# Three norms' rows on ScalarE, the key's gate as a scale of the turned probabilities, the feature shift on ScalarE

## The reference

```python
# part a: a state-space block, ends in a layer norm
y = y * silu(z)
y = y * rsqrt(mean(y * y) + EPS) * norm_w
y = einsum('bld,ed->ble', y, out_proj_w) + x
x = (y - mu) * rsqrt(var + EPS) * ln_w + ln_b        # "ln1"; the residual and "ln2" follow
# part b: attention, 8 heads of 64; the value is the one expert's whose gate is greatest,
# times that gate g[token, head]; the output is mixed by experts and scaled by the query's gate
out = softmax(q @ k.T * scale, causal) @ (g * v_expert)
x = layernorm(out_mixed + x)                           # "lnB"
# part c: linear attention with rotary angles
q, k = gelu(x @ Wq + bq) + 0.21, gelu(x @ Wk + bk) + 0.21
x = layernorm(rope(q) @ (rope(k).T @ v) / z + x) * gamma + beta   # "lnC"; residual and "lnD" follow
```

## Time and profile before

| | |
|---|---|
| median of 3 runs | 1579.16 us (1578.62 to 1583.59) |
| the profiled execution | 1580.04 us, its span 1578.1 us |
| mean granted TensorE clock | 0.974 |
| TensorE busy | 1438.5 us, 91% |
| VectorE busy | 1214.6 us, 77% |
| ScalarE busy | 820.8 us, 52% |
| GpSimd busy | 790.4 us, 50% |
| token stage, expert stage | 0 to 1068.6 us, 1068.6 to 1578.1 us |

### The profile page before, as it was taken

The page is one execution under the profiler, slowest core; times in us unless marked ns, Lnnn a source line. Parts: engine busy times, 40 slices in busy tenths (PEclk is TensorE's granted clock), DMA queues, the critical chain, the costliest instruction groups (busy, mean ns, idle before and its releaser), DMA issues. The chain is left out here.

```text
span 1578.1 us, 32322 instructions
## 1 busy us (share of the span) xinstructions
PE 1438.5 (91%) x10752; PEld 1261.2 (80%) x10752; DVE 1214.6 (77%) x2335; ACT 820.8 (52%) x1846; POOL 790.4 (50%) x1959
## 2 busy tenths in 40 slices
PE   5588999999999999999999999946999999869997
PEld 4366788788788788788788787836999999869997
DVE  4466798898898898898898887764888888736664
ACT  2234544544544544544544544303777776557774
POOL 0332253553553553553553552222777777557763
PEclk9998999999999999999999999966999999989999
DMA  6000000000000000000000000008676667877782
GB/s 236 7 7 1 8 1 14 15 1 14 15 1 15 15 1 14 15 1 15 15 1 15 8 1 8 8 7 252 171 197 188 185 186 199 254 266 301 300 316 71
DMA packets 140752, 132.10 MB, mean 84 GB/s; under 512 B 7376, under 2 KB 130512, under 8 KB 134096
## 3 DMA queue, kind: packets, MB, share of 16 engines
q1 hardware_dynamic: 140624, 130.50, 26.1%
HBM read 73.85 MB, written 56.62 MB: 83 GB/s over the span
## 5 line engine op out<-in xcount | busy, mean ns | idle before, releaser
L636 PE MATMUL bk<-ve_f,oe 128*128 128x128 f32 x2048 | 275.8, 279 | 0.8 <-DVE ve_f L1360 0.8
L636 PEld LDWEIGHTS bk<-ve_f,oe 128*128 128x128 f32 x2048 | 248.9, 192 | 23.4 <-issue 20.1
L2287 POOL TENSOR_TENSOR d_s<-d_ex 128x1024 f32<-128x1024 f32 x32 | 131.8, 4120 | 100.8 <-ACT d_ex L2087 100.8
L1360 DVE SCALAR_TENSOR_TENSOR ve_f<-ps_m,oT 128x512 f32<-128x512 f32 x248 | 166.3, 678 | 3.7 <-PE bk L636 2.3
L1321 DVE COPY_PREDICATED vals<-oh,bk 128x1024 f32<-128x1024 int32 x112 | 146.6, 1309 | 10.3 <-PE bk L404 8.5
L2037 PE MATMUL d_sl<-d_ex,e_prT 128*128 128x128 f32 x1024 | 136.0, 277 | 8.8 <-POOL d_ex L2304 8.8
L1971 PE MATMUL d_lg<-d_phf,d_xtf 128*128 (+1 forms) x1024 | 128.1, 287 | 14.4 <-DVE d_ex L2191 7.6
L1971 PEld LDWEIGHTS d_lg<-d_phf,d_xtf 128*128 128x128 f32 x1024 | 125.1, 203 | 15.2 <-issue 11.1
L2037 PEld LDWEIGHTS d_sl<-d_ex,e_prT 128*128 128x128 f32 x1024 | 125.4, 193 | 9.0 <-POOL d_ex L2304 9.0
L1981 PE MATMUL d_sl<-d_ex,d_xs 128*128 128x128 f32 x1024 | 121.3, 277 | 5.8 <-DVE d_ex L2202 5.8
L1981 PEld LDWEIGHTS d_sl<-d_ex,d_xs 128*128 128x128 f32 x1024 | 118.4, 194 | 6.2 <-DVE d_ex L2202 6.2
(11 more groups left out here) (340 smaller groups left out, 3730.5 us busy)
## 6 DMA issues: line engine op xcount, KB each, us to landing
logits<-d_raw SPq DMA_DIRECT2D x128, 256.0 KB, 3.3
e_lt<-logits SPq DMA_DIRECT2D x32, 1024.0 KB, 5.1
y_slots<-d_ys SPq DMA_DIRECT2D x64, 256.0 KB, 4.3
d_ex<-y_slots SPq DMA_DIRECT2D x16, 1024.0 KB, 6.8
d_w<-W SPq DMA_DIRECT2D x16, 256.0 KB, 3.4
oe<-xT SPq DMA_DIRECT2D x1, 2048.0 KB, 7.9
xt_in<-xT SPq DMA_DIRECT2D x16, 128.0 KB, 2.3
x_in<-x SPq DMA_DIRECT2D x16, 128.0 KB, 2.4
```

The lines of the kernel that those rows point to most:

```text
L636: last = pe.matmul(ps_u[:, cols], oe[:, hp, e, :], mo[:, n % MO, hp, :], start=False, stop=(e == NE - 1 and hp == HP - 1), skip_group_chec ...
L1360: V.scalar_tensor_tensor(mo[:, n % MO, :, :].rearrange("p a n -> p (a n)"), chosen_of(b, c), float(NE - e), oT[:, u, c, :, :].rearrange("p ...
L2287: G.tensor_tensor(s8[:], part[:, 0:8, :], part[:, 8:16, :], ALU.add).then_inc(n, 1)
```

## The change

The rows of three of the norms (ln1, lnB, lnC) are made by ScalarE. VectorE makes -mean * rstd (`shift`, one 128x2 instruction a norm), and ScalarE computes Identity(x * rstd + shift) in two instructions of 128x128. VectorE goes on with the product behind the rows when ScalarE has made them. The gate of the key isn't multiplied into vals by GpSimd (`b_vg` is gone) but is the scale of `b_pt`, which is now two instructions, 128x256 and 128x128. `c_q` is on ScalarE, behind the Gelus. Some buffers share space: sz is tz, yg is ya, and six buffers of the preparation lie in lx and mx; two waits move with that.

```diff
+        nb = {n: sb(f"{n}_b", [C]) for n in ("ln1", "lnB", "lnC")}
...
-        def scale_rows(dve, n, src, dst, b):
-            wait(dve, norms[n]["rstd"], RSQRT_OPS * (b + 1))
+        def shift(dve, n, b):
+            dve.wait_ge(norms[n]["rstd"], RSQRT_OPS * (b + 1))
+            dve.scalar_tensor_tensor(nb[n][:], nbuf[n][1][:, :, 0], -1.0, rstd_of(n)[:], ALU.mult, ALU.mult
+                                     ).then_inc(norms[n]["shift"], 1)
+        def scale_rows(act, n, src, dst, b):
+            act.wait_ge(norms[n]["shift"], b + 1)
             for c in range(C):
-                dve.tensor_scalar(dst[:, c, :], src[:, c, :], nbuf[n][1][:, c, 0:1], rstd_of(n)[:, c:c + 1],
-                                  ALU.subtract, ALU.mult).then_inc(norms[n]["rows"], 1)
+                nc.scalar.activation(dst[:, c, :], src[:, c, :], ACT.Identity, scale=rstd_of(n)[:, c:c + 1],
+                                     bias=nb[n][:, c:c + 1]).then_inc(norms[n]["rows"], 1)
...
@@ TensorE, b_pv @@
-                    pe.wait_ge(q["b_vg"], C * (b + 1))
+                    pe.wait_ge(q["b_v"], (NE - 1) * (b + 1))
...
@@ ScalarE @@
             def a_tz(b):
-                wait(act, q["a_sz"], b)
+                wait(act, q["a_yg"], b)
...
             def b_pt(b, h):
-                copy(pt[:, s, a, :, :].rearrange("p a b -> p (a b)"), ps_v[0][:, a, 0:3 * P]
-                     ).then_inc(q["b_pt"], 1)
+                nc.scalar.activation(pt[:, s, a, 0:2, :].rearrange("p a b -> p (a b)"), ps_v[0][:, a, 0:2 * P], ACT.Copy,
+                                     scale=gx[:, 0, h:h + 1])
+                nc.scalar.activation(pt[:, s, a, 2, :], ps_v[0][:, a, 2 * P:3 * P], ACT.Copy, scale=gx[:, 1, h:h + 1]
+                                     ).then_inc(q["b_pt"], 1)
...
+            def c_q(b):
+                act.wait_ge(q["c_g"], 2 * (b + 1))
+                wait(act, q["c_out_ps"], b)
+                nc.scalar.activation(ql[:], gl[:], ACT.Copy, bias=SHIFT).then_inc(q["c_q"], 1)
...
@@ ScalarE, slot @@
                     a_st(t)
                 if c:
+                    b_x2(t - 3, 1 - u)
                     b_x2t(t - 3, 1 - u)
...
                     c_gelu(t - 3)
+                    c_q(t - 3)
                 if more:
                     a_cin(t + 1, 0)
...
                     b_probs(t - 1, 3)
+                if a:
+                    a_na(t)
                 if more:
                     a_tz(t + 1)
...
                     b_probs(t - 1, 5)
+                if c:
+                    c_ncn(t - 3)
+                if b:
                     b_rgs(t - 1, 1)
...
@@ VectorE @@
             def a_y(b):
                 dve.wait_ge(q["a_y_ps"], b + 1)
+                wait(dve, q["a_sq"], C * b)
+                wait(dve, q["a_yt_ps"], b)
...
             def a_ln1(b):
-                scale_rows(dve, "ln1", ra, na, b)
                 dve.wait_ge(norms["ln1"]["rows"], C * (b + 1))
...
             def b_gate(b):
+                wait(dve, q["b_pt"], HB * b)
                 V.tensor_reduce(gx[:], g[:], AX.X, ALU.max).then_inc(n, 1)
...
             def c_ln(b):
-                scale_rows(dve, "lnC", rc2, ncn, b)
                 dve.wait_ge(norms["lnC"]["rows"], C * (b + 1))
...
@@ VectorE, slot @@
                     b_v(t - 1, 1)
                 if c:
-                    b_x2(t - 3, 1 - u)
+                    shift(dve, "lnB", t - 3)
...
                     b_v(t - 1, 6)
-                if c:
-                    c_q(t - 3)
...
                     b_max(t - 1, 1)
+                if a:
+                    shift(dve, "ln1", t)
                 if o:
                     b_mo(t - 2, u, 0, 7)
                 if a:
                     a_ln1(t)
...
                     b_mo(t - 2, u, 1, 1)
+                if c:
+                    shift(dve, "lnC", t - 3)
                 if b:
                     b_max(t - 1, 2)
                     b_rg(t - 1, 1)
...
@@ GpSimd, slot @@
                     rsqrt(pool, "rms", t, 1.0 / DI, EPS, q["a_sq"], C)
-                if b:
-                    b_vg(t - 1)
```

More of the change, by code:

```diff
@@ L117, in token_blocks @@
         causal_s = sb("causal_s", [P])
-        negb_f = sb("negb_f", [3, P])
         negb = sb("negb", [3, P], BF16)
@@ L129, in token_blocks @@
         in_w = sb("in_w", [2 * DI + 2 * D + NH])
-        out_w0 = sb("out_w0", [2, D])
         out_w = sb("out_w", [2, D])
@@ L165, in token_blocks @@
         bet = sb("bet", [D])
[L168 to L173, removed]
         ea = sb("ea", [NH])
@@ L190, in token_blocks @@
         mx = sb("mx", [C, NH, P])
+        lx_flat = lx[:, :, :, :].rearrange("p c h t -> p (c h t)")
+        mx_flat = mx[:, :, :, :].rearrange("p c h t -> p (c h t)")
+        sv, sa, su, sd, s2, sp = (lx_flat[:, TT * NH * i:TT * NH * (i + 1)].rearrange("p (n h) -> p n h", h=NH)
+                                  for i in range(6))
+        negb_f = mx_flat[:, 0:3 * P].rearrange("p (k n) -> p k n", k=3)
+        out_w0 = mx_flat[:, 3 * P:3 * P + 2 * D].rearrange("p (j d) -> p j d", j=2)
         ep = sb("ep", [NH])
@@ L195, in token_blocks @@
         tz = sb("tz", [C, DI])
-        sz = sb("sz", [C, DI])
+        sz = tz
         ya = sb("ya", [C, DI])
-        yg = sb("yg", [C, DI])
+        yg = ya
         sq = sb("sq", [DI])
@@ L285, in token_blocks @@
             a_op_ps a_r a_xb a_n a_x1t_ps a_x1h a_x1l a_x1
-            b_g_ps b_eg b_gate b_oht_ps b_oht b_qk_ps b_qk b_v_ps b_v0 b_v b_vg b_s_ps b_max b_p b_pt_ps b_pt
+            b_g_ps b_eg b_gate b_oht_ps b_oht b_qk_ps b_qk b_v_ps b_v0 b_v b_s_ps b_max b_p b_pt_ps b_pt
             b_pv b_rg b_rgs b_rgb_ps b_rgb b_ot b_m_ps b_mo b_oe b_oa b_oat_ps b_x2t_ps b_x2t b_start
@@ L290, in token_blocks @@
         q = {n: sem(n) for n in names}
-        norms = {n: {k: sem(f"{n}_{k}") for k in ("moments", "rstd", "rows")}
-                 for n in ("rms", "ln1", "ln2", "lnB", "lnC", "lnD")}
+        norms = {n: {k: sem(f"{n}_{k}") for k in ks.split()}
+                 for n, ks in (("rms", "rstd"), ("ln1", "moments rstd shift rows"), ("ln2", "moments rstd"),
+                               ("lnB", "moments rstd shift rows"), ("lnC", "moments rstd shift rows"),
+                               ("lnD", "moments rstd"))}
+        nb = {n: sb(f"{n}_b", [C]) for n in ("ln1", "lnB", "lnC")}
         nbuf = {n: (sb(f"{n}_st", [C, 6]), sb(f"{n}_mv", [C, 2]), sb(f"{n}_v", [C]), sb(f"{n}_h", [C]),
@@ L1052, in b_oa, with b_x2, a_na, c_ncn @@
                 copy(oa[:], ps_u).then_inc(q["b_oa"], 1)
+            def b_x2(b, u):
+                scale_rows(act, "lnB", rows_of(b).rearrange("p (c d) -> p c d", c=C), x2[:, u, :, :], b)
+            def a_na(b):
+                scale_rows(act, "ln1", ra, na, b)
+            def c_ncn(b):
+                scale_rows(act, "lnC", rc2, ncn, b)
             def b_x2t(b, u):
@@ L1173, in _ @@
             slot(NB // 2, 0, False, True, True, True, False)
+            b_x2(Y, 0)
             b_x2t(Y, 0)
             c_gelu(Y)
+            c_q(Y)
             b_oa(Z)
             c_kr(Y)
+            b_x2(Z, 1)
             b_x2t(Z, 1)
             c_gelu(Z)
+            c_q(Z)
+            c_ncn(Y)
             c_kr(Z)
             c_x3t(Y)
+            c_ncn(Z)
             c_x3t(Z)
@@ L1205, in a_sz @@
                 dve.wait_ge(q["a_tz"], b + 1)
-                wait(dve, q["a_yg"], b)
                 V.scalar_tensor_tensor(sz[:].rearrange("p c n -> p (c n)"), tz[:].rearrange("p c n -> p (c n)"), 1.0,
@@ L1252, in a_y @@
                 dve.wait_ge(q["a_y"], b + 1)
-                wait(dve, q["a_sq"], C * b)
-                wait(dve, q["a_yt_ps"], b)
                 V.tensor_tensor(yg[:], ya[:], sz[:], ALU.mult).then_inc(q["a_yg"], 1)
@@ L1370, in b_res @@
                 stats(dve, "lnB", b_rows(b), b)
[L1372 to L1379, removed]
             def c_v(b):
@@ L1647, in _ @@
             b_mo(Z, 1, 1, 3)
-            b_x2(Y, 0)
+            shift(dve, "lnB", Y)
             b_mo(Z, 1, 1, 4)
@@ L1652, in _ @@
             b_mo(Z, 1, 1, 7)
-            c_q(Y)
             c_v(Y)
@@ L1659, in _ @@
             c_res(Y, 0)
-            b_x2(Z, 1)
-            c_q(Z)
+            shift(dve, "lnB", Z)
+            shift(dve, "lnC", Y)
             c_v(Z)
@@ L1668, in _ @@
             rsqrt(dve, "lnC", Z, 1.0, 1e-12, norms["lnC"]["moments"], 2 * C)
+            shift(dve, "lnC", Z)
             c_ln(Z)
@@ L1693, in a_mx @@
                                     ALU.mult).then_inc(q["a_mx"], 1)
[L1695 to L1701, removed]
             def a_xb(b, u):
```

## The result

The changed kernel takes 1640.11 us (median of 4 runs, 1637.42 to 1641.69) against 1579.66 us before (4 runs): ratio 1.0376, 95% interval 1.0354 to 1.0399. It is slower by 60 us; the forecast was 1645, range 1612 to 1662.

A forecast was written before the change was run, and what follows sets the result against it. TensorE, busy 57.5 of 59.0 us in a steady slot, was taken as the bound. Profiled 1580.04 + 47.3 (thirteen slots' added waits) + 5.6 (other slots) + 12 (clock) = 1645 us, range 1612 to 1662.

The forecast's parts named there:

- steps 3, 5, 6: Steady slot: a_na behind b_probs(3) delays b_max(2), then c_ncn behind b_probs(5) delays b_max(3) and b_rgb(2): +3.64 us a slot.
- Step 1: c_q between the Gelus and a_cin on ScalarE: TensorE's second a_xbc waits, +0.26 us for all that follows.
- Step 4: On ScalarE tz, pt(2) and pt(3) come later; b_scores(2) waits for pt(3), putting TensorE at +1.45 us.
- Step 2: pt(1) ends 0.25 us later, b_scores(1) waits 0.2; b_max(1) moves no more than that, swallowed by the next step.
- step 5: c_ncn behind b_probs(5): VectorE's first c_ln product +3.64 us; rgS(1) behind it costs TensorE 0.7, pt(5) 0.2.
- The signs: 62 to 63 us slots, rgS waits near 1.8, b_scores(2) and VectorE waits 1.3 to 2.2, 1.2 GHz stretches, GpSimd 2 less.
- What costs nothing: lnB's rows on ScalarE, b_vg gone from GpSimd, the moved waits and shared buffers: no cost in a steady slot.
- The clock: Steady slots: TensorE's waits bring half-clock stretches, two slots in three at 1.4 us, +12 us; bounds 0 and 22.
- the rival that ended faster: VectorE, 0.85 us earlier at b_max(3), removes b_rgb(2)'s 0.82 us wait for rgS(2): 1569 us, chance 0.06.
- One link only: ScalarE reaches a_na or c_ncn earlier, or VectorE regains part: 1.5 to 2.5 us a slot, 1605 to 1618, chance 0.15.
- Nothing to measure: Moved work lies beside TensorE's 57.5 us and stalls fit the idle 1.5 us a slot: 1580 us, chance 0.05.
- the rival at 1633: The same waits as the forecast in all slots, but with the clock held at 2.4 GHz: 1633 us, chance 0.24.

The follow-up runs named there:

- e4_ncn_early: Changed kernel with c_ncn moved on ScalarE from behind b_probs(5) to ahead of b_probs(4), same work: 1601.98 us, 1.0127 of the kernel before.
- e1: Changed kernel with only ln1's rows back on VectorE: 1611.86 us, 1.0197 of the kernel before.
- e2: Changed kernel with only lnC's rows back on VectorE: 1606.83 us, 1.0162 of the kernel before.
- e5: Kernel before with only c_q moved to ScalarE, behind c_gelu: 1583.21 us, 1.0019 of the kernel before.
- e3: Changed kernel with both ln1's and lnC's rows back on VectorE: 1587.13 us, 1.0037 of the kernel before.
- e6: Kernel before with only the gate moved into b_pt (two instructions) and b_vg gone: 1587.96 us, 1.0054 of the kernel before.
- e8_beat: Kernel before with a_yt, c_kr ahead of b_probs(0), lnC's rows on ScalarE ahead of b_probs(4), b_max(3) one b_mo earlier: 1571.21 us, 0.9958.
- e9_order_only: Kernel before with a_yt, c_kr ahead of b_probs(0) and b_max(3) one b_mo earlier, lnC's rows on VectorE: 1573.66 us, 0.9953.

## Why the prediction was right

**The bound and the chain** (steps 3, 5, 6) hold to a tenth on VectorE and at b_rgb(2). Foretold for slot 10 in the old time scale, and measured less 36.13: na's product on VectorE 648.79, measured 648.85; b_max(2) 652.6, measured 652.57; the gamma product 656.23, measured 656.26; b_max(3) 661.5, measured 661.50; b_rgb(2) 664.7, measured 664.76; waits there 1.8, measured 1.76; pitch 62.7, measured 62.7. e4_ncn_early shows by experiment that it is the place of c_ncn that costs, and e1 and e2 that each norm has its own cost. That ln1's cost is its place too wasn't tried by moving it; it rests on the rows at 683.97, 684.06 and 684.98.

**The prices.** The Identity with two pointers took 0.454 us from PSUM and 0.50 from SBUF where 0.46 was taken; a pair 0.88 to 0.89 instead of 0.82; na's product came 0.06 later than foretold, and the starts behind it stay within 0.06 as well. b_pt is 0.480 and 0.372 against 0.476 and 0.370. c_q is 0.63, not 0.61.

**Step 1** foretold +0.26: TensorE's second a_xbc is at 668.99 - 36.13 = 632.86, against 632.59, and e5 gives 0.26. **Step 4** foretold b_scores(2) at +1.45: measured 686.74 - 36.13 = 650.61, +1.31, a tenth earlier, with no effect on VectorE, which came later anyway. **Step 2** foretold 0.2 us for b_scores(1). It starts 0.35 us later than before and the products ahead of it 0.26, so the step was worth 0.09. In **step 5** b_rgb(1) waited 0.43 and moved TensorE by 0.58, not 0.7. That TensorE stands at +2.7 ahead of b_rgb(2), near the foretold +2.6, is in part luck: steps 2, 4 and 5 gave less than their terms, and b_out's wait for mo, which the prediction doesn't have, moved it by 0.47. None of this reaches the pitch, because b_rgb(2) waits for rgS(2) anyway.

**The signs.** b_scores(2)'s new wait is 0.77 us, at most 0.9, and not 1.3 to 2.2; VectorE's two, 1.92 and 2.25, are as foretold. GpSimd is 3.0 us less busy a slot, not 2: b_vg took 2.0, and the small instructions of the Newton steps were recorded about 1 us shorter in total, which wasn't followed up.

**What costs nothing**: right for lnB with the shared buffers and moved waits (0.02 us a slot by e3, e5 and e6). For b_vg e6_gate_only speaks: it came out at +0.34, and no gain shows in it. lnC in e8_beat, ahead of b_probs(4), cost nothing either: 58.35 us a slot with its rows on ScalarE, 58.40 without. The rule of the Trainium skill (ScalarE: Activation LUTs, Rules for kernel authors) that adds and multiplies are VectorE's agrees with the single instructions here, 0.340 us on VectorE and 0.50 on ScalarE for the same 128x128. For the time of the kernel these runs bear it out where the piece stood behind the exponentials, and not where it stood ahead of them.

**Terms that were mis-sized.** The clock: I took 12 us; in the steady slots three stretches fell to 1.2 GHz, 64.35 - 62.71 = 1.64 each, 4.9 in all. I had 1.4 for one and took eight or nine of them. The number of falls was the term furthest off. One of them, with TensorE idle for half of the stretch before:

```profile
571.00:574.40 3.40, 1.65 (x16) 1.14 (x15) 2.93 (x9) 2.43 (x11) 0.38 (x2) 1.00 0.16 44
574.40:577.80 3.40, 3.40 (x19) 3.40 (x18) 2.63 (x8) 1.28 (x4) 0.00 (x0) 0.51 0.01 2
```

e1_ln1_back has the same wait of 1.8 us at b_rgb(2) in all its slots and no fall in any of them, so a wait of that length alone doesn't bring one. Against that, the other slots took 7.2 us (0 to 2) where I had 3.6: in slot 2 half clock lay over its first 9.9 us (below), and that isn't in my sum. Slot 15 grew by 2.3, not 3.64: I said it lacks only the start of the next block, but the second a_xbc and tz belong to that, and they carried step 1 and a part of step 4: b_scores(2) is 0.62 us late in slot 15, where it is 1.31 late in slot 10. Slot 16 and the last two blocks took 0.6, not 2.0. The expert stage is longer by 2.8 us with the same instructions, which I had at nothing; it has 46.0 us at half clock in this trace and 39.9 in that before. The errors have both signs, and the sum of 65 came out near 61.7. The middle of the forecast was right for its main term; that the total lies within 5 us owes something to errors that cancel.

**The rivals.** The change removes no wait: the rival that ended faster hung on rows being there by 646.9, and they came at 648.8. "One link only" would have shown 60.6 to 61.6 us a slot. "Nothing to measure" is out by 60 us. The clock wasn't held, but it fell rarely, so the result lies between the forecast and the rival at 1633; with the other slots 2.2 us and the expert stage 2.8 us over their terms, the rival that held the clock was nearer the truth in the steady slots than the forecast (4.9 us of falls, against 0 and 12).

## What to carry to other kernels

When an engine runs a fixed queue, a piece moved to it costs what stands before it in that queue, for everyone who waits for the piece; free capacity of the engine says nothing about that. Look for the place where the receiving engine already idles and the piece's inputs are ready: the same two instructions cost 2.2 us a slot less there. And before work is moved at all, try which wait one call earlier or later on the present engine removes; here that was the whole gain.

## What the runs showed of the hardware that I had not expected

**The clock ahead of slot 3 differs by more than the small moves cost.** In the trace of e8_beat slot 2 takes 55.4 us and in that of e9_order_only 58.1, though lnC's rows play no part in it. First e8_beat, then e9_order_only:

```profile
137.88:193.31 55.43, 54.04 (x384) 44.24 (x382) 45.19 (x90) 25.43 (x75) 15.86 (x52) 0.98 0.02 6
```

```profile
140.21:198.28 58.07, 56.68 (x384) 46.24 (x382) 45.24 (x90) 25.39 (x75) 15.86 (x52) 0.93 0.02 6
137.80:148.00 10.20, 9.89 (x34) 6.12 (x35) 4.26 (x9) 4.02 (x8) 0.00 (x0) 0.50 0.00 0
```

In the second trace TensorE ran at 1.2 GHz from 137.8 to 148 us and was busy for 9.89 of these 10.20 us. In the changed kernel it ran at 1.2 GHz for 20.5 us from 130.7 us on, busy for 18.26 of them. Over the twelve traces the time at half clock ahead of slot 3 adds up to between 6.8 us (e8_beat) and 23.9 us (e1_ln1_back), with 10.2 in the kernel before. This doesn't show that the kernels differ in it. Each trace is one execution, and executions of one kernel differ as well: those of e8_beat had a mean granted clock of 0.970 (1575.02 us) to 0.977 (1569.74 us, the one traced), and of e9_order_only the longest of six was traced. The expert stage, whose instructions are the same in all kernels, has the same spread: 502.2 us with 33.6 of them at half clock in e1_ln1_back, 508.0 us with 46.0 in the changed kernel. So some 3 us of a total belong to no part of the work, and 3 us is as much as c_q costs; for parts of that size the pitch is the better measure. What decides whether the clock falls there wasn't tried.

**Two pointers and the source.** The same Identity of 128x128 took 0.454 us with its source in PSUM and 0.50 us with its source in SBUF, in the means over all instructions. Copies of 128x512 in the same trace point the same way: 0.594 us from PSUM (cin, 32 of them) and 0.631 us from SBUF (ql, 16 of them). The pieces also run at different times and beside different work, and no run changes the source alone.
